# Loads ahead of their stage in a feed-forward and recurrent attention kernel

## The chip, the cores and the metric

The kernel runs on one core of a Trainium2 chip. Five engines work side by side, each through its own instruction queue in order: TensorE (PE, with its weight loads as PEld), VectorE (DVE), ScalarE (ACT), GpSimd (POOL), and SyncE (SP), which here only issues DMAs. They are ordered among each other by semaphores alone. The metric is the device time of one execution in microseconds (us), the median of several runs.

## What is computed

The input x is 4 x 1024 rows of 512 numbers. Two things are computed from its layer norm xn, and the output is x + s * silu(f):

```
xn = layernorm(x)
s  = gated delta rule attention: qkvz = xn @ w_qkvz.T, causal conv of 4 taps and silu on q, k, v,
     per head and step  S = S*exp(g); S += k (x) ((v - k@S)*beta); o = q@S
     s = rmsnorm(o * silu(z)) * norm_weight @ w_out.T
f  = feed-forward: routed = sigmoid(xn @ w_router + b_router) > 0.5
     h  = xn + (rmsnorm(xn)*n1 @ wv + bv) @ wo
     h2 = rmsnorm(h)*n2
     f  = where(routed, h + (silu(h2 @ w_gate) * (h2 @ w_up)) @ w_down, xn)
out = x + s * silu(f)
```

Everything is float32 but for some 16 bit intermediates in attention. The feed-forward width is 1408 (11 tiles of 128).

## The kernel before, in words

The program runs in two parts, one after the other. The functions are `feed_forward` and `attention`, both called from `program`.

**Feed-forward** works on 8 units of 512 rows (`UNITS_F`), each cut into 4 pieces of 128 rows (`NJ`). First the value and output weights are multiplied into one matrix (`pe_merge_weights`, L151 and L155 for the bias), which waits for both weights whole. Each unit then goes through an opening (`stats`, `normalise`, `router`: layer norm, mean square and router score, on VectorE), a front of three kinds of step per piece, and a back part. The front's steps are `columns` (PE transposes the normalised rows into `bank[0]`, ScalarE copies them out to `xt`, which also goes to DRAM for attention, L427), `attn` (PE multiplies by the merged matrix, L278; VectorE adds it into `h`, L288; ScalarE squares it, L297; GpSimd raises the mean to the power -1/2, L203) and `back` (VectorE scales the rows by that power, L304, in `dve_norm2`; PE transposes them, L313; VectorE evicts them into `h2t`, L322, and prepares `h`). The back part is 11 `gate` steps (gate product L347, silu on ScalarE L362, up product L352, product of both on VectorE L370) and 4 `down` steps (L383, selection on VectorE L392, silu L397, store to DRAM L457).

These steps are put into one list `order`, in which all engines work: the front of unit u is merged evenly with the gate steps of unit u - 1, and the down steps of unit u - 1 with the opening of unit u + 1. So in units 1 to 7 of the front, front steps and gate steps alternate; unit 0 has no gate steps to alternate with. Each engine runs its share of a step when it comes to it in the list. SP issues the loads and stores from a list of its own; it waits for a transfer or an engine where the code says so. At its end SP waits for its stores, the semaphores are cleared and all engines meet (L529).

**Attention** starts with a block of its own that loads three constants and fills `wlev` (L674 to L684). In the next block SP loads the first tile of columns, the small parameters, the weights of the first half of the heads in four kinds k, q, v, z (6 MB), the second tile and the output weights, and only then serves the loops. PE's first product there (L806) waits for tile 0 and the k weights. The order of all further work in this part comes from `planned`, a planner with a cost for every step (`TAKES`) and a due time for each; it runs 32 tiles of 256 rows (two groups of heads, four batches, four tiles). Row loads (`load_rows`) and stores serve the second group.

Of the kernel before, what the change touches and what calls it, by code (L numbers as in the profile page):

```python
# [99 lines left out]
def feed_forward(nc, bank, x, cst, w_router, b_router, norm1_w, wvt, bv, wo, norm2_w, w_gate, w_up, w_down, xt_d, g_d):  # L100


    with ExitStack() as ctx:
# [3 lines left out]
        def sem(name):  # L107
# [22 lines left out]
        sel = sb("sel", [P, 2, D])  # L130

        names = ["c_in", "r_in", "w_in", "g_in", "d_in", "z_set", "z_out", "h_set", "bvb", "wvo_ps", "wvo_sb", "cb_ps", "cb_sb",
                 "x_in0", "x_in1", "x_in2", "x_in3", "stat", "mvs", "var", "rst", "xnd", "sqd", "scr", "r1a", "r1d", "rtd", "kpt", "xc",
                 "trx", "xtd", "xt_out", "a_ps", "h_sb", "sq_sb", "r2a", "r2d", "h2s", "trh", "h2td", "xk", "hk",
                 "g_ps", "u_ps", "g_act", "hid_sb", "d_ps", "selw", "g_done", "g_out0", "g_out1"]
        s = {n: sem("f_" + n) for n in names}
        first, last = s[names[0]].num, s[names[-1]].num
# [20 lines left out]
        def act_merge_weights(act):  # L158
            act.wait_ge(s["c_in"], 16 * (1 + len(small)))
# [4 lines left out]
        def dve_spread_bias(dve):  # L164
            dve.wait_ge(s["c_in"], 16 * (1 + len(small)))
# [81 lines left out]
        def pe_columns(pe, u, j):  # L247

            n = NJ * u + j
            if n == 0:  # L250
                pe.wait_ge(s["c_in"], 16 * (1 + len(small)))
# [143 lines left out]
        def act_select(act, u, j):  # L395
# [4 lines left out]
        front = [("columns", 0), ("columns", 1), ("attn", 0), ("columns", 2), ("attn", 1), ("columns", 3), ("back", 0), ("attn", 2), ("back", 1), ("attn", 3),  # L400
                 ("back", 2), ("back", 3)]
        order = [(step, 0) for step in (("stats",), ("normalise",), ("router",))]
# [1521 lines left out]
```

## Time and profile before

| | |
|---|---|
| median of 3 runs | 4777.71 us (4777.23 to 4779.94) |
| profiled execution | 4782.79 us, span 4781.0 us |
| PE busy | 4586.8 us (96%) |
| PE weight loads | 3134.5 us (66%) |
| VectorE busy | 2680.7 us (56%) |
| ScalarE busy | 2348.9 us (49%) |
| GpSimd busy | 1387.1 us (29%) |
| mean granted clock of PE | 0.991 |
| HBM traffic | 79.09 MB read, 34.11 MB written, 24 GB/s over the span |

How the rows are read. A row of a timeline has the start in us, the duration in us, the engine (SPq is SP's DMA issues), the line of the kernel, the operation, output and inputs, shapes, and xN where N instructions of a kind are merged; in brackets stands the idle time of the engine before it and what ended that. A row of waits names the engine and line that waited, what for, the total in us, the number of waits and the longest. A window row has the stretch, its length, then busy us and number of instructions of PE, PEld, DVE, ACT and POOL, the granted PE clock (1.00 is full speed, 2.4 GHz, and 0.50 the lower of the two levels, 1.2 GHz), the mean busy share of the 16 DMA engines, and GB/s. The granted clock at the very start of the trace is shown as 1.00 until the first change is recorded. Ends of matmuls are modelled: each is shown a little longer than its slot. SP's duration is that of the issue; the landing is listed apart.

### The profile page before, as it was taken

The page shows a single profiled execution, that of the slowest core. Times are in us where ns is not written, and L with a number is a line of the kernel's source. Part 1 is how long each engine was busy: PE and PEld are TensorE (multiplying, and loading weights), DVE is VectorE, ACT ScalarE, POOL GpSimd, SP SyncE. Part 2 cuts the span into 40 slices and gives each one's busy share as a digit, 9 for nine tenths or more (in the row PEclk, how much of TensorE's full clock was granted, in tenths as well). Part 3 has the DMA queues.
Part 4 walks back from the last instruction along what each step waited for, and adds up shares of the span by engine and source line. Part 5 has one row for each costly group of instructions (what it writes and reads, how often), then busy time and mean ns, then how long its engine had stood idle before and what let it go on. Part 6 is the DMA issues. An engine that isn't in the chain of part 4 may idle for free.

```text
span 4781.0 us, 81715 instructions
## 1 busy us (share of the span) xinstructions
PE 4586.8 (96%) x30056; PEld 3134.5 (66%) x30056; DVE 2680.7 (56%) x6818; ACT 2348.9 (49%) x5714; POOL 1387.1 (29%) x1542
## 2 busy tenths in 40 slices
PE   7999999997899999999999999999999999999998
PEld 3444444443777777777777777777777777777775
DVE  3222222212666666666666666666676666667664
ACT  1000111101566656666666666666666666666664
POOL 1000000000233333333333333333343333434333
PEclk9999999998999999999999999999999999999998
DMA  3000000002000000000000001100000000010000
GB/s 132 19 27 25 22 24 27 18 9 94 6 10 10 10 12 10 10 10 10 10 10 17 10 28 45 34 23 23 29 26 23 23 23 23 23 37 23 23 19 30
DMA packets 72605, 118.46 MB, mean 25 GB/s; under 512 B 12432, under 2 KB 29456, under 8 KB 72208
## 3 DMA queue, kind: packets, MB, share of 16 engines
q1 hardware_dynamic: 72208, 113.22, 7.1%
q8 instruction: 242, 3.96, 0.4%
q14 instruction: 155, 1.27, 0.1%
HBM read 79.09 MB, written 34.11 MB: 24 GB/s over the span
## 4 chain that ended last, share of the span: by engine, by line
PE 63%; DVE 10%; issue 1%; ACT 1%; POOL 0%; SPq 0%; DMA 0%; DVEq 0%; POOLq 0%; ACTq 0%
PE bank L806 18%; PE bank L810 10%; PE bank L1169 9%; PE bank L1448 7%; DVE vraw L836 3%; PE bank L1086 2%; PE bank L1342 2%; PE bank L1356 2%; PE bank L1382 2%; PE bank L1294 2%; PE bank L1317 2%; PE bank L1070 1%; PE bank L945 1%; PE bank L1071 1%; PE bank L812 1%
## 5 line engine op out<-in xcount | busy, mean ns | idle before, releaser
L806 PE MATMUL bank<-xtile,wt 128*128 128x259 f32 x4096 | 1083.0, 396 | 79.2 <-DVE vraw L836 50.9
L806 PEld LDWEIGHTS bank<-xtile,wt 128*128 128x128 f32 x4096 | 725.5, 191 | 214.3 <-DVE vraw L836 81.1
L1228 ACT ACTIVATE xyinv<-bank 128x512 f16<-128x512 f32 x768 | 457.4, 596 | 365.0 <-PE bank L1169 362.5
L1206 DVE TENSOR_TENSOR wlev<-bank,mask 128x256 f16<-128x256 f32 x768 | 320.9, 420 | 469.6 <-PE bank L1169 467.0
L1448 PE MATMUL bank<-wot,xnt 128*128 128x512 f32 x1024 | 532.8, 611 | 0.9 <-ACT xnt L1441 0.8
L810 PE MATMUL bank<-wt,xtile 128*128 128x512 f32 x1024 | 523.4, 617 | 0.0
L836 DVE SCALAR_TENSOR_TENSOR vraw<-bank,taps,vraw 128x256 f32<-128x256 f32 x768 | 370.2, 482 | 126.7 <-ACT vraw L829 105.5
L370 DVE TENSOR_TENSOR hid<-bank,gate 128x512 f32<-128x512 f32 x88 | 60.9, 692 | 521.1 <-PE bank L352 521.1
L1146 POOL TENSOR_TENSOR kend<-ktok,bend 128x256 f32<-128x256 f32 x256 | 158.6, 640 | 636.3 <-issue 635.8
L1169 PEld LDWEIGHTS bank<-xyinv,lth 128*128 128x128 f16 x3584 | 220.7, 98 | 167.3 <-issue 108.5
L347 PE MATMUL bank<-h2t,wg_sb 128*128 128x512 f32 x704 | 318.4, 595 | 0.0
L352 PE MATMUL bank<-h2t,wu_sb 128*128 128x512 f32 x704 | 316.5, 592 | 0.0
L383 PE MATMUL bank<-wd_sb,hid 128*128 128x512 f32 x704 | 303.5, 592 | 0.9 <-DVE hid L370 0.9
L1121 POOL TENSOR_TENSOR ltm<-ltm,mask 128x512 f32<-128x512 f32 x128 | 148.2, 1158 | 501.5 <-DVE ltm L1104 501.5
L1169 PEld LDWEIGHTS bank<-wlev,xyinv 128*128 128x128 f16 x3072 | 187.1, 99 | 144.7 <-issue 95.0
L1169 PE MATMUL bank<-xyinv,lth 128*128 128x64 f16 (+1 forms) x3584 | 265.1, 197 | 0.9 <-ACT xyinv L1228 0.9
L829 ACT ACTIVATE vraw<-bank,taps 128x256 f32<-128x256 f32 x256 | 121.6, 475 | 282.7 <-PE bank L806 279.8
L1055 POOL TENSOR_TENSOR gm<-con,gdec 128x512 f32<-128x512 f32 x128 | 133.6, 1044 | 401.5 <-PE bank L1086 315.5
L352 PEld LDWEIGHTS bank<-h2t,wu_sb 128*128 128x128 f32 x704 | 133.8, 190 | 168.4 <-issue 168.4
L383 PEld LDWEIGHTS bank<-wd_sb,hid 128*128 128x128 f32 x704 | 133.1, 190 | 166.2 <-issue 166.2
L362 ACT ACTIVATE gate<-bank 128x512 f32<-128x512 f32 x88 | 52.6, 598 | 360.1 <-PE bank L347 360.1
L347 PEld LDWEIGHTS bank<-h2t,wg_sb 128*128 128x128 f32 x704 | 130.7, 191 | 146.0 <-issue 146.0
(179 smaller groups left out, 9327.0 us busy)
## 6 DMA issues: line engine op xcount, KB each, us to landing
xtile<-xt_scratch SPq DMA_DIRECT2D x32, 518.0 KB, 4.1
xn<-x SPq DMA_DIRECT2D x32, 256.0 KB, 5.3
xt_scratch<-xt SPq DMA_DIRECT2D x8, 1024.0 KB, 5.8
g_scratch<-sel SPq DMA_DIRECT2D x32, 256.0 KB, 2.0
wt<-w_qkvz SPq DMA_DIRECT2D x4, 2048.0 KB, 13.2
part_scratch<-prow SPq DMA_DIRECT2D x32, 256.0 KB, 2.1
prow<-part_scratch SPq DMA_DIRECT2D x32, 256.0 KB, 2.7
grow<-g_scratch SPq DMA_DIRECT2D x32, 256.0 KB, 3.5
```

What stands on the lines that cost most here:

```text
L347: i = pe.matmul(bank[2 + f % 2][:], wg_sb[:, k, f * P:(f + 1) * P], h2t[:, u % 2, k, :], start=(k == 0), stop=(k == KT - 1))
L352: i = pe.matmul(bank[4 + f % 2][:], wu_sb[:, k, f * P:(f + 1) * P], h2t[:, u % 2, k, :], start=(k == 0), stop=(k == KT - 1))
L383: i = pe.matmul(bank[6 + j % 2][:], hid[:, f, j * P:(j + 1) * P], wd_sb[:, f, :], start=(f == 0), stop=(f == FT - 1))
L806: j = pe.matmul(b_p[:, 0:WIN], wt[:, k, c:c + P], xtile[:, par, k, :], **st)
L810: j = pe.matmul(b_p[:], xtile[:, par, k, HALO + cc * P:HALO + (cc + 1) * P], w, **st)
L836: dve.scalar_tensor_tensor(out=acc, in0=tile_bank("product", prod_of[i])[:, tap:tap + TILE], scalar=taps[:, group(q), i, tap:tap + 1], in1 ...
L1121: pool.tensor_tensor(ltm[:], ltm[:], mask[:, M_NEG, :].unsqueeze(1).broadcast_to([P, HEADS, P]), ALU.subtract).then_inc(s["lti_sb"], 1)
L1146: i = pool.tensor_tensor(kend[:, r * REP:(r + 1) * REP], ktok[:, tile % 2, cc, m * KPB + r].unsqueeze(1).broadcast_to([P, REP, P]), bend[: ...
L1169: i = pe.matmul(dst[:, h * cols:(h + 1) * cols], lhsT(h), rhs(h), start=start and h == 0, stop=stop, skip_group_check=True)
L1206: dve.tensor_tensor(wlev[:, lv - 1].rearrange("p h (b t s) -> p h b t s", t=2, s=z)[:, :, :, 0, :], b_inv[p][:, 0:HEADS * P // 2].rearrang ...
L1228: act.activation(dst, b_inv[p][:].rearrange("p (a h b s) -> p a h b s", a=2, h=HEADS, s=z), ACT.Copy).then_inc(s[f"xy_sb{p}"], 1)
L1448: i = pe.matmul(b_o[:], xnt[:, h], wot[:, h], start=(h == 0), stop=(h == GV - 1))
```

## The change

- A set of tiles and semaphores that attention needs (`resident`) is now allocated around both parts: constants, masks, `nw`, the qkvz weights `wt`, two tiles of columns, `sel`, and the small parameters. The gate and up weights lie in the memory of `wt`, the value and output weights in that of `hid`, and attention's `xrow` and `grow` in that of `sel`.
- Value and output weights come in four slices of rows each, as the first DMAs; each slice pair has a semaphore `w_in{e}`. The three small vectors are issued after the first pair, and the load of x after the last. The merge runs over slices on the outside, so that all four banks finish during the last slice.
- Attention's constants are loaded right after x, its small parameters during unit 0, tiles 0 and 1 of the columns at the beginning of the last round of SP's loop (when all columns are in DRAM), and the weights of the first half after the last up product (`u_ps`), beside the last down products.
- The scaling of the rows (`dve_norm2`) is a step `scale` of its own, put right behind `attn`, and the front's order relative to the gate steps is written out by hand.
- The semaphore clear and the barrier between the parts are gone; so are SP's waits for its stores (row loads of the second group wait for `g_out`), and the block for the constants. VectorE makes its constants at the head of its attention program; GpSimd waits for them (`c_set`), and PE before the first level step with `lv == 1`.

```diff
+def resident(nc, ctx):
+    shapes = {"con": ([P, N_CONST, P], F32), "mask": ([P, N_MASK, P], F16), "nw": ([P, 1], F32), "wt": ([P, KT, GROWS], F32), "xtile": ([P, 2, KT, WIN], F32), "sel": ([P, 2, D], F32),
+              "wba": ([P, KT, GROUPS, 4 * GK], F32), "taps": ([P, GROUPS, 4 * GK, TAPS], F32), "dtb": ([P, GROUPS, GV], F32), "neg_a": ([P, GROUPS, GV], F32)}
+    r = {name: ctx.enter_context(nc.sbuf_tensor(name, shape, dtype)) for name, (shape, dtype) in shapes.items()}
+    for name in ("c_in", "wk_in", "wq_in", "wv_in", "wz_in", "wba_in", "small_in", "x_in0", "x_in1", "g_out0", "g_out1"):
+        r[name] = ctx.enter_context(nc.semaphore("a_" + name))
+    return r
...
+def load_weights(sp, r, w_qkvz, g, kind):
+    lo, hi = W_SPANS[kind]
+    sp.dma_start(r["wt"][:, :, lo:hi], w_qkvz[:, g * GROWS + lo:g * GROWS + hi].rearrange("(k p) n -> p k n", p=P)).then_inc(r[f"w{kind}_in"], 16)
+def load_columns(sp, r, xt_d, q):
+    b, i = divmod(q % HALF_TILES, TPB)
+    sp.dma_start(r["xtile"][:, q % 2], xt_d[:, :, b * PADT + i * TILE:b * PADT + i * TILE + WIN]).then_inc(r[f"x_in{q % 2}"], 16)
...
-        ident, zero = sb("f_ident", [P, P]), sb("f_zero", [P, D])
-        wvt_sb, wo_sb, bvb = sb("wvt_sb", [P, KT, D]), sb("wo_sb", [P, KT, D]), sb("bvb", [P, KT, P])
+        ident, zero = r["con"][:, C_ID, :], sb("f_zero", [P, D])
-        wg_sb, wu_sb = sb("wg_sb", [P, KT, FF]), sb("wu_sb", [P, KT, FF])
+        both = r["wt"][:].rearrange("p k n -> p (k n)")
+        wg_sb, wu_sb = (both[:, i * KT * FF:(i + 1) * KT * FF].rearrange("p (k f) -> p k f", k=KT) for i in range(2))
...
+        wvt_sb, wo_sb = hid[:, 0:KT, :], hid[:, KT:2 * KT, :]
+        sel = r["sel"]
...
         def pe_merge_weights(pe):
-            pe.wait_ge(s["w_in"], 32)
-            for k in range(KT):
-                for e in range(KT):
+            for e in range(KT):
+                pe.wait_ge(s[f"w_in{e}"], 32)
+                for k in range(KT):
                     i = pe.matmul(bank[2 + k][:], wvt_sb[:, e, k * P:(k + 1) * P], wo_sb[:, e, :], start=(e == 0), stop=(e == KT - 1))
-                i.then_inc(s["wvo_ps"], 1)
+                    if e == KT - 1:
+                        i.then_inc(s["wvo_ps"], 1)
...
-        front = [("columns", 0), ("columns", 1), ("attn", 0), ("columns", 2), ("attn", 1), ("columns", 3), ("back", 0), ("attn", 2), ("back", 1), ("attn", 3),
-                 ("back", 2), ("back", 3)]
+        front = ["gate", "gate", ("columns", 0), ("columns", 1), "gate", ("attn", 0), ("scale", 0), ("columns", 2), "gate", "gate", ("back", 0), ("attn", 1), ("scale", 1),
+                 ("columns", 3), "gate", "gate", ("back", 1), ("attn", 2), ("scale", 2), "gate", "gate", ("back", 2), ("attn", 3), ("scale", 3), "gate", "gate", ("back", 3)]
         for u in range(UNITS_F + 1):
-            lists = []
-            if u < UNITS_F:
-                lists.append([(step, u) for step in front])
-            if u:
-                lists.append([(("gate", f), u - 1) for f in range(FT)])
-            order += merged(*lists)
-            lists = []
-            if u:
-                lists.append([(("down", j), u - 1) for j in range(NJ)])
-            if u + 1 < UNITS_F:
-                lists.append([(step, u + 1) for step in (("stats",), ("normalise",), ("router",))])
-            order += merged(*lists)
+            f = 0
+            for step in front:
+                if step != "gate" and u < UNITS_F:
+                    order.append((step, u))
+                elif step == "gate" and u:
+                    order.append((("gate", f), u - 1))
+                    f += 1
+            order += merged([(("down", j), u - 1) for j in range(NJ)] if u else [], [(step, u + 1) for step in opening] if u + 1 < UNITS_F else [])
...
+                for e in range(KT):
+                    sp.dma_start(wvt_sb[:, e, :], wvt[e * P:(e + 1) * P, :]).then_inc(s[f"w_in{e}"], 16)
+                    sp.dma_start(wo_sb[:, e, :], wo[e * P:(e + 1) * P, :]).then_inc(s[f"w_in{e}"], 16)
+                    if e == 0:
+                        for dst, src in small:
+                            sp.dma_start(dst, src).then_inc(s["c_in"], 16)
                 load(0)
-                sp.dma_start(ident[:], cst[:, C_ID, :]).then_inc(s["c_in"], 16)
-                for dst, src in small:
-                    sp.dma_start(dst, src).then_inc(s["c_in"], 16)
+                load_constants(sp, r, cst, masks, norm_weight)
...
-                sp.dma_start(wvt_sb[:], kp(wvt)).then_inc(s["w_in"], 16)
-                sp.dma_start(wo_sb[:], kp(wo)).then_inc(s["w_in"], 16)
-                sp.wait_ge(s["w_in"], 32)
+                for e in range(KT):
+                    sp.wait_ge(s[f"w_in{e}"], 32)
+                sp.wait_ge(s["x_in3"], 16)
                 sp.dma_start(wg_sb[:], kp(w_gate)).then_inc(s["g_in"], 16)
                 sp.dma_start(wu_sb[:], kp(w_up)).then_inc(s["g_in"], 16)
                 load(1)
                 sp.wait_ge(s["g_in"], 32)
...
                 columns_out(0)
-                sp.wait_ge(s["d_in"], 16)
+                load_small(sp, r, conv_w, dt_bias, a_log, w_ba)
                 sp.wait_ge(s["z_set"], 1)
                 for dst, src in zeros:
                     sp.dma_start(dst, src).then_inc(s["z_out"], 16)
...
+                    if u == UNITS_F:
+                        sp.wait_ge(s["z_out"], 16 * len(zeros))
+                        sp.wait_ge(s["xt_out"], 16 * UNITS_F)
+                        for q in range(2):
+                            load_columns(sp, r, xt_d, q)
+                        sp.wait_ge(s["u_ps"], FT * UNITS_F)
+                        for kind in "kqvz":
+                            load_weights(sp, r, w_qkvz, 0, kind)
                     for j in range(NJ):
                         sp.wait_ge(s["g_done"], NJ * (u - 1) + j + 1)
                         row = (u - 1) * FTILE + j * P
                         sp.dma_start(g_d[row:row + P, :], sel[:, j % 2, :]).then_inc(s[f"g_out{j % 2}"], 16)
-                sp.wait_ge(s["z_out"], 16 * len(zeros))
-                sp.wait_ge(s["xt_out"], 16 * UNITS_F)
-                for p in range(2):
-                    sp.wait_ge(s[f"g_out{p}"], 8 * NJ * UNITS_F)
...
+                    elif kind == "scale":
+                        dve_norm2(dve, u, *i)
                     elif kind == "back":
-                        dve_norm2(dve, u, *i)
                         dve_back(dve, u, *i)
                         dve_keep(dve, u, *i)
...
-        nc.gpsimd.sem_clear(range(first, last + 1))
-        nc.all_engine_barrier()
...
+        def dve_constants(dve):
+            dve.memset(mhalf[:], -0.5).then_inc(c_set, 1)
+            for lv in range(LEVELS - 1):
+                dve.tensor_copy(wlev[:, lv], mask[:, M_ID, :].unsqueeze(1).broadcast_to([P, HEADS, P])).then_inc(c_set, 1)
+            dve.wait_ge(c_set, LEVELS)
...
             if lv == 1:
                 pe.wait_ge(s[f"y1_sb{p}"], u + 1)
+            if n == 0 and lv == 1:
+                pe.wait_ge(c_set, LEVELS)
...
+            if c == HALF_CHUNKS:
+                for p in range(2):
+                    sp.wait_ge(s[f"g_out{p}"], 8 * CHUNKS // GROUPS)
...
-                load_tile(sp, 0)
-                load_small(sp)
-                load_products(sp, 0, "kqvz")
-                load_tile(sp, 1)
                 load_out(sp, 0)
...
+                pool.wait_ge(c_set, LEVELS)
                 for kind, *i in order["pool"]:
```

The functions `load_constants` and `load_small` of the new version issue the same DMAs as the lines L674 to L676 and L691 to L694 of before. The attention functions take their tiles from `resident`; nothing else in them differs.

## Rows read from the trace of the kernel before

**Rows 1.** Windows by stage, all engines.
```profile
0.00:16.76 16.76, 0.00 (x1) 0.01 (x1) 7.60 (x22) 0.00 (x0) 2.03 (x8) 1.00 0.63 208
16.76:70.08 53.32, 39.94 (x108) 19.03 (x109) 19.75 (x43) 9.08 (x17) 10.81 (x16) 0.91 0.62 212
70.08:1138.80 1068.72, 1034.87 (x2557) 463.47 (x2556) 233.79 (x458) 109.67 (x204) 74.04 (x110) 1.00 0.06 21
1138.80:1161.83 23.03, 0.15 (x2) 0.04 (x1) 2.30 (x9) 2.13 (x3) 0.00 (x0) 0.57 0.49 125
1161.83:4781.00 3619.17, 3511.80 (x27392) 2651.98 (x27392) 2417.23 (x6288) 2227.98 (x5490) 1300.20 (x1408) 0.99 0.07 22
```

**Rows 2.** Waits of PE from 64 to 1150 us: total, times, longest.
```profile
PE bank L313 <- DVE h L304: 33.0, 28, 1.2
```

**Rows 3.** Timeline from 0 to 39 us, DVE, PE and SP.
```profile
0.73 1.81 SPq L422 DMA_DIRECT2D xn<-x  x4
...
7.57 2.46 DVE L210 BATCH_NORM_STATS2 stats<-xn 128x6 f32<-128x512 f32 x4
...
11.90 1.91 DVE L222 TENSOR_SCALAR xn<-xn,mv,rstd 128x512 f32<-128x512 f32 x4 [1.58 <-POOL rstd L179]
...
16.76 16.84 PE L151 MATMUL bank<-wo_sb,wvt_sb 128*128 128x512 f32 x32 [16.76 <-DMA wo_sb<-wo]
...
36.87 0.60 PE L256 MATMUL bank<-f_ident,xn 128*128 128x128 f32 x4
...
37.07 0.69 DVE L170 COPY cbias<-bank 128x512 f32<-128x512 f32 x1 [17.11 <-PE bank L155]
...
38.71 3.60 PE L278 MATMUL bank<-wvo,xt 128*128 128x512 f32 x8
```

**Rows 4.** DMA issues from 0 to 9 us: count, KB each, us to landing.
```profile
xn<-x SPq DMA_DIRECT2D x4, 256.0 KB, 3.4
```

**Rows 5.** Windows in two other cuts, all engines.
```profile
69.00:73.60 4.60, 4.42 (x9) 2.36 (x10) 4.25 (x13) 1.88 (x2) 0.00 (x0) 0.50 0.01 4
...
1160.00:1180.00 20.00, 16.69 (x62) 12.86 (x63) 9.12 (x20) 5.55 (x9) 0.00 (x0) 0.85 1.04 399
```

**Rows 6.** Timeline of the end of unit 0.
```profile
53.44 3.60 PE L278 MATMUL bank<-wvo,xt 128*128 128x512 f32 x8
...
57.18 0.75 DVE L288 SCALAR_TENSOR_TENSOR h<-bank,r,h 128x512 f32<-128x512 f32 x1 [1.66 <-PE bank L278]
...
59.04 0.55 POOL L203 TENSOR_TENSOR r<-r,mhalf 128x1 f32<-128x1 f32 x1
...
69.17 1.11 PE L256 MATMUL bank<-f_ident,xn 128*128 128x128 f32 x4 [6.67 <-DVE xn L222]
```

**Rows 7.** Timeline of one stall in unit 1's front.
```profile
253.97 3.60 PE L352 MATMUL bank<-h2t,wu_sb 128*128 128x512 f32 x8
...
258.22 0.48 DVE L304 TENSOR_SCALAR h<-h,r 128x512 f32<-128x512 f32 x1
...
258.75 0.66 PE L313 MATMUL bank<-f_ident,h 128*128 128x128 f32 x4 [1.18 <-DVE h L304]
...
259.44 0.69 DVE L322 TENSOR_TENSOR h2t<-bank,n_sb 128x512 f32<-128x512 f32 x1 [0.75 <-PE bank L313]
```

**Rows 8.** Timeline of SP, two stores of columns.
```profile
251.36 0.52 SPq L427 DMA_DIRECT2D xt_scratch<-xt  x1
...
387.49 0.52 SPq L427 DMA_DIRECT2D xt_scratch<-xt  x1
```

**Rows 9.** Timeline from the last down products to the first attention product.
```profile
1100.94 38.01 PE L383 MATMUL bank<-wd_sb,hid 128*128 128x512 f32 x88 [0.87 <-DVE hid L370]
...
1140.53 0.32 SPq L457 DMA_DIRECT2D g_scratch<-sel  x1
...
1143.63 0.33 SPq L674 DMA_DIRECT2D con<-cst  x1
...
1161.83 5.79 PE L806 MATMUL bank<-xtile,wt 128*128 128x259 f32 x16 [22.88 <-DMA wt<-w_qkvz]
```

More of the change, by code:

```diff
@@ L129, in feed_forward @@
         hid = sb("hid", [P, FT, FTILE])
-        sel = sb("sel", [P, 2, D])
-        names = ["c_in", "r_in", "w_in", "g_in", "d_in", "z_set", "z_out", "h_set", "bvb", "wvo_ps", "wvo_sb", "cb_ps", "cb_sb",
+        wvt_sb, wo_sb = hid[:, 0:KT, :], hid[:, KT:2 * KT, :]
+        sel = r["sel"]
+        names = ["c_in", "r_in", *(f"w_in{e}" for e in range(KT)), "g_in", "d_in", "z_set", "z_out", "h_set", "bvb", "wvo_ps", "wvo_sb", "cb_ps", "cb_sb",
                  "x_in0", "x_in1", "x_in2", "x_in3", "stat", "mvs", "var", "rst", "xnd", "sqd", "scr", "r1a", "r1d", "rtd", "kpt", "xc",
                  "trx", "xtd", "xt_out", "a_ps", "h_sb", "sq_sb", "r2a", "r2d", "h2s", "trh", "h2td", "xk", "hk",
-                 "g_ps", "u_ps", "g_act", "hid_sb", "d_ps", "selw", "g_done", "g_out0", "g_out1"]
+                 "g_ps", "u_ps", "g_act", "hid_sb", "d_ps", "selw", "g_done"]
         s = {n: sem("f_" + n) for n in names}
-        first, last = s[names[0]].num, s[names[-1]].num
+        s.update({n: r[n] for n in ("g_out0", "g_out1")})
         kp = lambda a: a.rearrange("(k p) n -> p k n", p=P)
@@ L158, in act_merge_weights @@
         def act_merge_weights(act):
-            act.wait_ge(s["c_in"], 16 * (1 + len(small)))
+            act.wait_ge(s["c_in"], 16 * len(small))
             for k in range(KT):
@@ L250, in pe_columns @@
             if n == 0:
-                pe.wait_ge(s["c_in"], 16 * (1 + len(small)))
+                pe.wait_ge(r["c_in"], 48)
             pe.wait_ge(s["xnd"], n + 1)
@@ L591, in merged, with attention @@
     return [step for _, _, step in sorted(at, key=lambda x: x[:2])]
-def attention(nc, bank, x, cst, masks, w_qkvz, w_ba, conv_w, dt_bias, a_log, norm_weight, w_out, xt_d, g_d, part_d, out):
+def attention(nc, bank, r, x, w_qkvz, w_out, xt_d, g_d, part_d, out):
     with ExitStack() as ctx:
@@ L628, in attention @@
         xnt = sb("xnt", [P, GV, P])
-        xrow, grow, prow = sb("xrow", [P, D]), sb("grow", [P, D]), sb("prow", [P, D])
+        xrow, grow, prow = r["sel"][:, 0, :], r["sel"][:, 1, :], sb("prow", [P, D])
         pout, yout = prow, grow
@@ L1466, in pool_out @@
             pool.wait_ge(s["po_sb"], c + 1)
-            pool.tensor_tensor(yout[:], pout[:], grow[:], ALU.mult).then_inc(s["yg_sb"], 1)
+            pool.tensor_tensor(yout, pout[:], grow, ALU.mult).then_inc(s["yg_sb"], 1)
             pool.wait_ge(s["yg_sb"], c - HALF_CHUNKS + 1)
-            pool.tensor_tensor(yout[:], yout[:], xrow[:], ALU.add).then_inc(s["yo_sb"], 1)
+            pool.tensor_tensor(yout, yout, xrow, ALU.add).then_inc(s["yo_sb"], 1)
         def rows(c):
@@ L1476, in load_rows @@
             sp.wait_ge(s["stored"], 16 * c)
-            for dst, src in ((prow, part_d), (grow, g_d), (xrow, x)):
-                sp.dma_start(dst[:], src[rows(c), :]).then_inc(s["rows_in"], 16)
+            if c == HALF_CHUNKS:
+                for p in range(2):
+                    sp.wait_ge(s[f"g_out{p}"], 8 * CHUNKS // GROUPS)
+            for dst, src in ((prow[:], part_d), (grow, g_d), (xrow, x)):
+                sp.dma_start(dst, src[rows(c), :]).then_inc(s["rows_in"], 16)
         def store(sp, c):
@@ L1485, in store @@
                 sp.wait_ge(s["yo_sb"], c - HALF_CHUNKS + 1)
-                sp.dma_start(out[rows(c), :], yout[:]).then_inc(s["stored"], 16)
+                sp.dma_start(out[rows(c), :], yout).then_inc(s["stored"], 16)
         unit_lanes, tile_lanes = {}, {}
@@ L1811, in _ @@
             def _(dve):
+                dve_constants(dve)
                 dve_rates(dve)
@@ L1878, in program @@
         bank = [ctx.enter_context(nc.psum_tensor(f"bank{i}", [P, 512], F32)) for i in range(8)]
-        feed_forward(nc, bank, x, cst, w_router, b_router, norm1_w, wvt, bv, wo, norm2_w, w_gate, w_up, w_down, xt_d, g_d)
-        attention(nc, bank, x, cst, masks, w_qkvz, w_ba, conv_w, dt_bias, a_log, norm_weight, w_out, xt_d, g_d, part_d, out)
+        r = resident(nc, ctx)
+        feed_forward(nc, bank, r, x, cst, masks, w_qkvz, w_ba, conv_w, dt_bias, a_log, norm_weight,
+                     w_router, b_router, norm1_w, wvt, bv, wo, norm2_w, w_gate, w_up, w_down, xt_d, g_d)
+        attention(nc, bank, r, x, w_qkvz, w_out, xt_d, g_d, part_d, out)
 _INS = ["w_qkvz", "w_ba", "conv_w", "dt_bias", "A_log", "norm_weight", "w_out"]
```

73 lines of the change are left out of this document (29 added, 44 removed).

## The prediction

> **What bounds the kernel now.** I read the busy time by stage first. [rows 1] cut the span at five points: the wait for the first weights, unit 0 of the feed-forward part, its units 1 to 7, the change from one part to the other, and attention. TensorE (PE) is busy for 1034.87 of 1068.72 us in units 1 to 7 and for 3511.80 of 3619.17 us in attention, so it is the bound in both, and time is won only where it stands still: 16.76 us at the start, 13.4 us in unit 0, about 34 us in the units and 22.9 us at the change. The waits say what these are. In the units nearly all of it is one wait, the transposes of the scaled rows (L313) for the scaling of them (L304), 33.0 us in 28 pieces [rows 2]. The timelines of the start, of unit 0, of one such stall and of the change carry the four terms below.
>
> **Term 1, the start.** PE merges the value and output weights from 16.76, when both megabytes have landed, and reaches the first column transposes (call them c0) at 36.87: 20.1 us, of which some 3 are the half clock of its first matmuls (32 in 16.84 us [rows 3], against the 0.43 us each of term 3). The change issues the first slice pair as the first two DMAs, and the merge goes slice by slice. The four loads of x, 256 KB each as every slice is, went out at 0.73 [rows 3] and took 3.4 us from issue to landing [rows 4]; so the first pair, issued by about 1.2, lands near 4.3 with the count of its semaphore. If no later slice is late, c0 comes at 4.3 + 20.1 = 24.4, 12.5 us earlier. A slice pair feeds PE for 3.4 us at full clock and 6.9 at half; the last is needed near 17. At the poorest rate of a row, 208 GB/s over the whole start [rows 1], 2.1 MB are there by 11. So the slices are not the limit. x now comes behind them: 3.1 MB are there by 16 at 208 GB/s, and by 9 at the 399 GB/s of the weight stream at the change [rows 5]; I take 12. VectorE then needs 0.6 us for the last statistics, 1.9 from there to the first normalised row (7.57 + 2.46 to 11.90), and 8.1 from that to the end of the router work (11.90 to 19.96, which is 37.07 less its 17.11 of idle time), after which it copies the bias that the first value/output product (a0) needs [rows 3]. That is 23 at my value, hidden by the merge, and 27 at the poor rate, which would put a0 at 28 in place of 26.2. Term: -12.5, with -10.7 and -13 as ends. The gate and up weights are asked for when slices and x have landed, near 13 where it was 16.7, and are needed at 56: covered.
>
> A page speaks against this part. The Trainium skill ("DMA: Bandwidth & Descriptors", Rules for kernel authors) advises transfers of a megabyte or more and calls those below 64 KB mostly overhead; the eight slices are 256 KB, where there were two of 1 MB. Taken at the 138 GB/s that its table has for 64 KB, as an estimate, the 2 MB would need 15 us and the last slice would still come about when PE asks for it. The x loads of the same size, down in 3.4 us [rows 4], show nothing of such a rate.
>
> **Term 2, unit 0.** Without gate steps to lie between, moving the scaling ahead has a price here: VectorE and PE now do product, row scaling and back-transpose strictly one after the other. From the rows of the last product: start of the product to VectorE's update 3.74 us (53.44 to 57.18), to the end of the power on GpSimd 2.41, hand-over 0.05, scaling to the transposes 0.53 (258.22 to 258.75), transposes 0.50 (0.66 less a tail of 0.16): 7.2 us for each of four [rows 6, 7]. The last transposes start at 28.4 after a0; 0.69 to the eviction, 0.69 in it (259.44) and 0.1 more, and unit 0's first gate product can start: 29.9 after a0. Before, a0 at 38.71 to unit 1's first columns at 69.17 is 30.5, and PE was then at half clock until 73.6, which cost another 2.2 us: 32.7 [rows 3, 6]. The wait for unit 1's normalised rows (6.67) is gone, since two gate steps of 6.9 us now lie ahead of those columns, where VectorE needs 4.3 us to its first normalised row (7.57 to 11.90) and a little more for what it still has of unit 0. The clock decides what remains. In the chain PE idles about 3 us after each 3.9 of work; in the trace it was down after the 6.67 us wait (0.50 at 69 to 73.6 [rows 5]) and stood at 0.91 on average over 16.76 to 70.08, in which PE was busy for three quarters [rows 1]. Between no loss and every matmul of the stage at half clock (16 us of work, +16, and 2 in the first gate) I take 4, nearer to none, since no idle stretch here is half as long as that wait. Term: 29.9 + 4 - 32.7 = +1.2, from -3 to +15.
>
> The Trainium skill ("TensorE: Matmul & The Clock Gate", HAM oscillation) describes such a loop, bursts of matmuls with waits between, as one that falls back to half clock at every wait and pays for it in each burst. By that rule the stage would lie at the upper end, and it is a rival below.
>
> **Term 3, units 1 to 7.** A unit takes 136.13 us (251.36 to 387.49 from one store of columns to the next) [rows 8]. The up product of 253.97 has 8 matmuls of 0.43 us (38.01 less 3.60 over 80 more of them [rows 7, 9]) and a modelled tail of 0.16; its slot ends at 257.41; the transposes start at 258.75. VectorE does the product with the gate (it waits for that same up product), and only then the scaling: 1.34 us, four times a unit. In the new order the scaling stands right behind the value/output product, with two gate steps before its transposes, so it is ready (3.3 us after the product's end against 13.8): -5.36 a unit. New is, first, that the columns 0 and 1 stand side by side and share a bank: from the first of them to the product behind both 1.84 us (36.87 to 38.71 [rows 3]), where two sets of four transposes without a wait would take 0.92 (0.60 and 0.66 in the rows, less the tail: taken as 0.46 each), +0.92. Second, the down products wait for the last gate product's eviction; in the last unit that showed as 0.87 of idle time and the tail of 0.16 [rows 9]; with 0.46 of transposes between, +0.57. The wait that VectorE gains at each scaling is 1.7 us (57.18 + 0.75 to 59.6); behind it stands the product with the gate for a step that PE ends 7 us after the value/output product, so some 4 us of slack remain, and ScalarE's squares and GpSimd's power have nothing long ahead of them. Unit: 132.26. Term: 7 x -3.87 = -27.1. Ends: -29 (the transposes lose their slow start too, 0.03 to 0.06 each) and 0 (rival).
>
> **Term 4, the change.** PE's last down product ends at 1138.8 and the first attention product starts at 1161.83. What lies between: the last selection and its store (issued until 1140.85), its landing, a semaphore clear with two barriers, constants from 1143.63, then tile, small loads and weights one after another [rows 9]. All of these loads now are issued before: constants at the start, small ones in unit 0, two tiles after unit 6's stores, and 6 MB of weights once the last gate step is through, a microsecond before the down products' start at 1100.94. At 399 GB/s [rows 5] they take 16 us, beside down products of 38.01 us. Stores of the selection are queued behind them on SP; the buffer of the first is needed again by the third selection, three of four down products or 28.5 us later: free. What stays is selection, ScalarE, the last store's issue and the block's exit; by the rows that is 1140.85 plus part of the 2.8 us to 1143.63, a landing and a clear now left out. I take 1141.7 (1141.1 to 1144): PE starts 20.1 earlier. VectorE's constants (they are within the 2.30 us of its work in this stretch [rows 1]) run beside the first product. That product ran at half clock, 16 matmuls in 5.79 us, where full clock would need some 3.4 (an estimate: 259 columns against the 512 of 0.43 us); after 3 us instead of 23 of idle time the clock may hold, worth 0 to 2.5, taken as 1. Term: -21.1.
>
> **At nothing:** eleven more small issues of SP in the first 60 us (SP has no one waiting until 115); `sel` as home of `xrow` and `grow`; the waits on g_out, long fulfilled at chunk 32; the planner's order, whose costs are untouched. Uncovered, the SP issues would cost 6 us.
>
> **Sum.** -12.5 + 1.2 - 27.1 - 21.1 = -59.5 us. The profiled execution took 4782.79 (span 4781.0), so it would take 4723.3; it lay 5.1 above the median of 4777.71, and the median comes to **4718**.
>
> **Rivals.**
> 1. The clock falls in each wait of unit 0 and stays down into attention (for: by the rows of term 2 PE is idle nearly half of the stage; against: work of 3.9 us between). +12 from term 2, +1 from term 4: 4731. Chance 0.15.
> 2. The start stays bound by loads: x behind the weights, or slices trickling in (for: 208 GB/s; against: 3.4 us landings). Half to all of term 1 goes: 4724 to 4731. Chance 0.08.
> 3. The moved scaling does not free PE: VectorE's new 1.7 us waits push the gate evictions late, so that term 3 is lost and 28 x 0.4 us come on top (for: VectorE is strictly in order; against: 4 us of slack). 4718 + 27 + 11 = 4756. Chance 0.06.
> 4. The change of parts is only half closed, because stores sit behind 6 MB or the exit costs more: 4725. Chance 0.05.
> 5. Slower than before: attention itself paces differently with its tiles at other places in memory. It has 3619 us [rows 1]; it decides from 59.5 us, 1.6% of that, 1.9 us in each of 32 tiles. Nothing in the profile speaks for it: same instructions, same order. At 2.5% it would give 4808. Chance 0.03.
> Forecast: 0.63, for itself 4709 to 4727.
>
> **Numbers.** The range takes in rivals 1, 2 and 4: 4704 to 4736, which leaves out 3 and 5 and about a tenth on the edges. 0.2%, the least that can be told from no change here, is 9.6 us. Faster 0.96, same 0.01, slower 0.03.
>
> **What would show it.** PE's first matmul near 4.3 and c0 near 24.4 (term 1); unit 0's first gate product near 56 to 62, with the granted clock of 26 to 60 above 0.8 (term 2); no wait of L313's successor on the scaling in units 1 to 7, one of 0.8 us for ScalarE's columns instead, and 132.3 us between stores of columns (term 3); some 3 us between the last down product and the first attention product (term 4); attention within 5 us of 3619. Wrong would be it with a first matmul after 8, a unit above 134, or an attention stage longer by more than 10 us.

## The result, and the profile after

The changed kernel takes 4718.83 us (median of 4 runs, 4716.38 to 4724.52); in the same comparison the kernel before takes 4777.48 us. The ratio is 0.9878, with an interval of 0.9861 to 0.9895. The forecast was 4718. The two profiled executions took 4782.79 and 4719.77 us, a difference of 63.0: the one of before lay 5.3 us above its median, the one of after 0.9. So the terms below add up to 63 us, not to 59.

Lines of the kernel after that the rows name: L190 is the merge and L195 its bias, L296 the transposes of the columns and L304 ScalarE's eviction of them, L318 the value/output product, L344 the scaling, L353 the transposes of the scaled rows and L362 their eviction, L387 the gate and L392 the up product, L410 the product of both, L423 the down products, L455 the feed-forward block itself, L824 attention's first products. In kernels that the experiments edit, some of these stand one or two lines lower.

The windows of the kernel after, cut as in [rows 1] (wait for the first weights, unit 0, units 1 to 7 with the last down products, the change, attention):

```profile
0.00:4.22 4.22, 0.00 (x0) 0.00 (x0) 0.00 (x0) 0.00 (x0) 0.75 (x6) 1.00 0.50 130
4.22:57.79 53.57, 40.32 (x105) 18.44 (x105) 22.81 (x51) 10.04 (x18) 10.81 (x16) 0.97 0.84 278
57.79:1100.00 1042.21, 1032.30 (x2560) 466.56 (x2560) 238.94 (x471) 107.43 (x203) 75.32 (x112) 1.00 0.08 28
1100.00:1102.46 2.46, 0.00 (x0) 0.03 (x1) 0.87 (x3) 0.82 (x2) 0.00 (x0) 0.97 0.04 14
1102.46:4718.00 3615.54, 3505.92 (x27392) 2647.63 (x27392) 2418.52 (x6295) 2229.01 (x5492) 1300.35 (x1408) 0.99 0.06 20
```

PE's idle time went from 16.8 to 4.2 us at the start, from 34 to 10 us in the units and from 22.9 to 2.5 us at the change. In unit 0 it stayed at 13. The three largest waits of PE from 60 to 1115 us, engine and line, what for, total, number and longest:

```profile
PE bank L296 <- ACT xt L304: 5.9, 7, 0.9
PE bank L423 <- DVE hid L410: 3.9, 8, 0.9
PE bank L824 <- PEq L455: 2.5, 1, 2.5
```

The 33.0 us of [rows 2] are gone altogether. In their place stand the two small waits that the prediction named, on ScalarE's columns (L296, seven times) and on the last gate product's eviction (L423), and the exit of the feed-forward block (L455). The timeline of the kernel after, start and unit 0:

```profile
4.22 16.88 PE L190 MATMUL bank<-hid 128*128 128x512 f32 x32 [4.22 <-DMA hid<-wo]
...
5.91 2.30 SPq L460 DMA_DIRECT2D xn<-x  x4
...
11.86 2.73 DVE L250 BATCH_NORM_STATS2 stats<-xn 128x6 f32<-128x512 f32 x4 [6.68 <-DMA xn<-x]
...
13.96 0.38 SPq L480 DMA_DIRECT2D wt<-w_gate  x1
...
24.37 0.60 PE L296 MATMUL bank<-con,xn 128*128 128x128 f32 x4
24.57 0.69 DVE L210 COPY cbias<-bank 128x512 f32<-128x512 f32 x1
...
26.22 3.60 PE L318 MATMUL bank<-wvo,xt 128*128 128x512 f32 x8
...
32.96 0.66 PE L353 MATMUL bank<-con,h 128*128 128x128 f32 x4 [2.71 <-DVE h L344]
33.45 5.29 PE L318 MATMUL bank<-wvo,xt 128*128 128x512 f32 x8
...
42.39 3.60 PE L318 MATMUL bank<-wvo,xt 128*128 128x512 f32 x8
...
49.12 0.66 PE L353 MATMUL bank<-con,h 128*128 128x128 f32 x4 [3.13 <-DVE h L344]
49.61 3.60 PE L318 MATMUL bank<-wvo,xt 128*128 128x512 f32 x8
...
57.79 5.39 PE L387 MATMUL bank<-h2t,wt 128*128 128x512 f32 x8 [0.78 <-DVE h2t L362]
```

And from the timeline of the same execution, two stores of columns one unit apart, then the change:

```profile
238.09 0.52 SPq L465 DMA_DIRECT2D xt_scratch<-xt  x1
...
370.37 0.52 SPq L465 DMA_DIRECT2D xt_scratch<-xt  x1
...
1061.12 2.38 SPq L128 DMA_DIRECT2D wt<-w_qkvz  x4
...
1061.96 38.01 PE L423 MATMUL bank<-wd_sb,hid 128*128 128x512 f32 x88 [0.87 <-DVE hid L410]
...
1102.46 5.35 PE L824 MATMUL bank<-xtile,wt 128*128 128x259 f32 x16 [2.49 <-PEq L455]
```

| term | forecast | measured | from |
|---|---|---|---|
| 1, start | -12.5 | -12.5 | first columns at 24.37, before 36.87 |
| 2, unit 0 | +1.2 | +0.7 | 31.57 + 1.8 of half clock in the first gate product, against 32.7 |
| 3, units | -27.1 | -27.0 | 132.28 us a unit, before 136.13 |
| 4, change | -21.1 | -20.4 and -3.6 | down products to first attention product 40.50, before 60.89; attention 3615.54, before 3619.17 |

### The profile page after: what moved, and what is told of

It is laid out like the page before. It is cut to its first block and busy times, and to the rows that moved or that the text cites. A ratio compares the mean times of both kernels' runs of the same rounds, so it can differ in the third digit from the quotient of the medians.

```text
span 4718.0 us, 81696 instructions
## 1 busy us (share of the span) xinstructions
PE 4578.5 (97%) x30056; PEld 3132.7 (66%) x30056; DVE 2681.1 (57%) x6818; ACT 2347.3 (50%) x5714; POOL 1387.2 (29%) x1542
## 5 line engine op out<-in xcount | busy, mean ns | idle before, releaser
L824 PE MATMUL bank<-xtile,wt 128*128 128x259 f32 x4096 | 1080.0, 396 | 58.8 <-DVE vraw L854 50.5
L824 PEld LDWEIGHTS bank<-xtile,wt 128*128 128x128 f32 x4096 | 723.7, 191 | 192.6 <-DVE vraw L854 80.8
L828 PE MATMUL bank<-wt,xtile 128*128 128x512 f32 x1024 | 523.4, 617 | 0.0
L410 DVE TENSOR_TENSOR hid<-bank,gate 128x512 f32<-128x512 f32 x88 | 60.9, 692 | 485.5 <-PE bank L392 485.5
L387 PE MATMUL bank<-h2t,wt 128*128 128x512 f32 x704 | 318.3, 595 | 0.8 <-DVE h2t L362 0.8
L392 PE MATMUL bank<-h2t,wt 128*128 128x512 f32 x704 | 316.5, 592 | 0.0
L423 PE MATMUL bank<-wd_sb,hid 128*128 128x512 f32 x704 | 304.0, 593 | 3.9 <-DVE hid L410 3.9
L423 PEld LDWEIGHTS bank<-wd_sb,hid 128*128 128x128 f32 x704 | 133.1, 190 | 170.7 <-issue 170.7
L392 PEld LDWEIGHTS bank<-h2t,wt 128*128 128x128 f32 x704 | 133.8, 190 | 168.4 <-issue 168.4
L387 PEld LDWEIGHTS bank<-h2t,wt 128*128 128x128 f32 x704 | 132.7, 191 | 159.9 <-issue 158.9
```

The lines of the kernel that those rows point to most:

```text
L387: i = pe.matmul(bank[2 + f % 2][:], wg_sb[:, k, f * P:(f + 1) * P], h2t[:, u % 2, k, :], start=(k == 0), stop=(k == KT - 1))
L392: i = pe.matmul(bank[4 + f % 2][:], wu_sb[:, k, f * P:(f + 1) * P], h2t[:, u % 2, k, :], start=(k == 0), stop=(k == KT - 1))
L423: i = pe.matmul(bank[6 + j % 2][:], hid[:, f, j * P:(j + 1) * P], wd_sb[:, f, :], start=(f == 0), stop=(f == FT - 1))
L824: j = pe.matmul(b_p[:, 0:WIN], wt[:, k, c:c + P], xtile[:, par, k, :], **st)
L828: j = pe.matmul(b_p[:], xtile[:, par, k, HALO + cc * P:HALO + (cc + 1) * P], w, **st)
```

## The experiments

All of them are edits of the changed kernel. Their medians are set beside its 4718.83, but they were taken in three comparisons, each with its own runs of the kernel before: 4783.19 us beside `late_weights`, `x_first`, `whole_first` and `scale_in_back`, 4778.76 beside `old_front`, `unit0_order`, `columns_apart` and `warm`, 4778.0 beside the rest. The first of these is 5.7 us above the 4777.48 of the result, so differences of medians of a few microseconds carry little. Of the edited kernels all but `scale_in_back`, `old_front` and `both_orders` have ratios whose intervals meet the 0.9861 to 0.9895 of the changed kernel; for those the reading rests on the rows of one profiled execution each.

**The scaling and the order (terms 2 and 3).** `scale_in_back` keeps the hand-written front and moves only the scaling back into the `back` step:

```
-                    elif kind == "scale":
-                        dve_norm2(dve, u, *i)
                     elif kind == "back":
+                        dve_norm2(dve, u, *i)
```

> The changed kernel with the scaling of the rows done at the head of the back step again; the hand-written order of the front is kept. My theory: what paid in units 1 to 7 is that the scaling no longer stands behind the product with the gate; so the stall of 1.34 us comes back four times a unit, a unit takes 137.6 instead of 132.27 us, unit 0 stays as it is (nothing stands between there), and the time is 4718.8 + 37.5 = 4756. Rival (the gain comes from the new order, two gate steps ahead of each back step): no change within 3 us.

It took 4754.52 us (ratio to before 0.9945, 0.993 to 0.9959). The waits of PE and two stores of columns of this kernel:

```profile
PE bank L353 <- DVE h L344: 36.1, 29, 3.1
```

```profile
111.67 0.52 SPq L465 DMA_DIRECT2D xt_scratch<-xt  x1
...
248.86 0.52 SPq L465 DMA_DIRECT2D xt_scratch<-xt  x1
```

The stall is back (33 us in 28 pieces and one of 3.1 that belongs to unit 0), and a unit takes 137.19 us. The order alone gives nothing; in it a unit is even 1.06 us longer than before, with the new wait on ScalarE's columns (7 times 0.84 us in its waits) as the largest part. The 0.4 us a unit that I expected too much is the wait before the down products (L423): its waits show it once, in the last unit, where the kernel after has it eight times.

`old_front` restores order and scaling of before, and leaves the early loads in:

```
-            f = 0
-            for step in front:
-                ...
+            lists = []
+            if u < UNITS_F:
+                lists.append([(step, u) for step in front])
+            ...
```

> The changed kernel with the order of the feed-forward steps and the scaling inside the back step as they were before; all early loads and the sliced merge stay. My theory (terms 2 and 3 are the order's alone, and the early loads have no part in them): a unit takes 136.1 us instead of 132.27, 27 us in all, and unit 0 is a little shorter, by 0.7 us between its first value/output product and its first gate product at full clock: 4718.8 + 27.0 - 0.7 = 4745. Rival (the terms are not additive, part of the gain of the order came from earlier loads): 4735 or less.

4745.69 us (0.9931, 0.9916 to 0.9945), a unit 136.14. So terms 2 and 3 together are 26.9 us in medians, and they do not lean on the early loads.

`unit0_order` gives unit 0 a list of its own:

```
+        first = [("columns", 0), ("columns", 1), ("attn", 0), ("scale", 0), ("columns", 2), ("attn", 1), ("columns", 3),
+                 ("back", 0), ("scale", 1), ("attn", 2), ("back", 1), ("scale", 2), ("attn", 3), ("back", 2), ("scale", 3), ("back", 3)]
...
-            for step in front:
+            for step in (front if u else first):
```

> The changed kernel with a list of its own for unit 0: product 1 ahead of back 0, product 2 ahead of back 1, product 3 ahead of back 2, each scaling ahead of the transposes by one product. My theory: the price of unit 0 is a chain of four times product, scaling, transposes, 7.2 us each; with products between, only the last stall of 2.8 us is left, the first gate product comes 20.4 us after the first value/output product instead of 31.6, and the clock does not fall: 4718.8 - 11.2 - 1.5 = 4706. Rival (unit 0 is bound by loads or by what VectorE has to do for unit 1, so that the wait moves behind it): 4715 to 4719.

4707.31 us (0.9851, 0.9836 to 0.9866). PE in the timeline of this kernel, from the first value/output product to the first gate product:

```profile
25.52 3.60 PE L318 MATMUL bank<-wvo,xt 128*128 128x512 f32 x8
...
44.82 0.66 PE L353 MATMUL bank<-con,h 128*128 128x128 f32 x4 [3.21 <-DVE h L344]
46.27 5.35 PE L387 MATMUL bank<-h2t,wt 128*128 128x512 f32 x8 [0.78 <-DVE h2t L362]
```

20.75 us instead of 31.57, one stall on the scaling instead of four. The clock half of the expectation failed in one place: all four products run at full clock, but the first gate product still does not (5.35 us for 8 against 3.60).

`columns_apart` puts a gate step between columns 0 and columns 1:

```
-        front = ["gate", "gate", ("columns", 0), ("columns", 1), "gate", ...
+        front = ["gate", ("columns", 0), "gate", ("columns", 1), "gate", ...
```

> The changed kernel with a gate step between columns 0 and columns 1 (gate, columns 0, gate, columns 1, gate, ...). My theory: the wait of PE for ScalarE's eviction of the shared bank, 0.9 us in each of seven units, goes: 4718.8 - 6.3 = 4712.5. Rival (unit 1's first rows are not normalised after one gate step, and the wait comes back there): up to 3 us of it return, 4715.5.

4713.75 us (0.9863, 0.9848 to 0.9878). A unit takes 131.22 us (239.55 to 370.77 between stores of columns), 1.06 less, 7.4 in all; no wait came back in unit 1. The median alone, 5.1 us lower, could not show it. Its timeline holds one row that the kernel after does not have:

```profile
26.03 3.67 PE L318 MATMUL bank<-wvo,xt 128*128 128x512 f32 x8 [1.20 <-DVE cbias L210]
```

Here the bias was late. VectorE copied it at 25.20, 0.6 us later than in the kernel after, because x landed later (its first use is at 12.67, in the kernel after at 11.86); and the merge took 15.39 us instead of 16.88, so PE was ready 1.5 us earlier (first columns at 22.82). x, behind the slices, held PE up by 1.2 us in this execution.

**The start (term 1).** `x_first` issues x and the small vectors ahead of the slices, `whole_first` keeps the weights first but as two loads of 1 MB:

```
 x_first:                                       whole_first (the merge waits for w_in0 alone):
+                load(0)                        +  sp.dma_start(wvt_sb, kp(wvt)).then_inc(s["w_in0"], 16)
+                for dst, src in small: ...     +  sp.dma_start(wo_sb, kp(wo)).then_inc(s["w_in0"], 16)
                 for e in range(KT): ...        -  for e in range(KT): ...
-                load(0)                           load(0)
```

> The changed kernel with x and the small vectors issued ahead of the eight weight slices. My theory: slicing and order each carry a part of term 1. The first slice pair is issued at about 5.4 and lands near 8.7, so the merge starts 4.5 us later than at 4.22, the first column transposes come near 28.9 and the time is 4723.3. Rival a: order is everything (x ahead costs the whole 12.5 us): merge at 16.7, 4731. Rival b: slices behind x trickle in and stop the merge in between: merge starts near 9 but takes more than the 16.9 us of before.

> The changed kernel with value and output weights as two loads of 1 MB, still the first to be issued; the merge keeps its loop over slices but waits once for both. My theory: at about 400 GB/s both are there near 8.5, so the merge starts 4.3 us later than with slices and the time is 4723.1. Rival (large transfers run so much faster that slicing wins nothing): both land by 5.5, 4720 or less. If they land as slowly as in the kernel before (8.7 and 10.8 us from issue) the merge starts at 12 and the time is 4726.5.

4727.05 us (0.9886, 0.987 to 0.9903) and 4724.17 us (0.9884, 0.9869 to 0.9899). The merge in the timeline, of `x_first` and of `whole_first`:

```profile
8.53 16.34 PE L190 MATMUL bank<-hid 128*128 128x512 f32 x32 [8.53 <-DMA hid<-wo]
```

```profile
8.99 16.77 PE L190 MATMUL bank<-hid 128*128 128x512 f32 x32 [8.99 <-DMA hid<-wo]
```

The merge starts 4.3 us later behind x and 4.8 us later with whole weights; both were expected at 4.3 to 4.5. The columns follow at 28.14 and 29.04. The rest of term 1 (16.76 to about 8.8) comes with either of the two alone. `x_first` is 8 us slower in its median and not 4. The clock of unit 0 (below) may be a part: from its first value/output product to the first gate product it took 33.74 us, `whole_first` 31.57. The kernel before in the same comparison, 5.7 us above its other median, may be another: by the ratio to it, `x_first` would be at 4723.0 on the scale of the result, where 4723.3 was expected.

The 2 MB are there at 8.99 in two pieces. In eight pieces the last, issued at 5.43, took 5.7 us and was there at 11.1; the merge, which needs it last, ran 16.88 us and was not stopped. The Trainium skill ("DMA: Bandwidth & Descriptors", Rules for kernel authors) asks for a megabyte or more per transfer where the greatest bandwidth is the aim. The 11.1 against 8.99 does not speak against that, though three small loads stood among the slices and no run separates the causes. Here a smaller first piece decided, and the rate of the whole did not.

**The change (term 4).** `late_weights` loads tiles and weights at the head of attention again; `late_both` also the small parameters:

```
-                load_small(sp, r, conv_w, dt_bias, a_log, w_ba)        # late_both only
-                        ...
-                        for q in range(2):
-                            load_columns(sp, r, xt_d, q)
-                        ...
-                            load_weights(sp, r, w_qkvz, 0, kind)
 (attention)
+            load_columns(sp, r, xt_d, 0)
+            load_small(sp, r, conv_w, dt_bias, a_log, w_ba)        # late_both only
+            for kind in "kqvz":
+                load_weights(sp, r, w_qkvz, 0, kind)
+            load_columns(sp, r, xt_d, 1)
```

> The changed kernel with the two column tiles and the 6 MB of attention weights loaded at the head of attention again; constants and small parameters stay early, the clear and the barrier stay out. My theory: the change of parts was bound by a chain in which the weights were only the last link (issue to first product 6.2 us in the kernel before, 1155.60 to 1161.83); so the first attention product comes about 6.7 us later than in the changed kernel, near 3 + 6.7 us after the last down product, and the time is 4725.5. Rival a: the weights were the whole of it, 20 us, then 4739. Rival b: taking out barrier, clear and constants was all, then 4719.

> The changed kernel with the column tiles, the weights and also the small parameters loaded at the head of attention, in the order of the kernel before. My theory: the loads stand in one chain on SP, so that the nine small issues (5.9 us from 1149.67 to 1155.56 in the kernel before) add to what the late weights alone showed (9.27 us of idle time ahead of the first attention product): 15.2 us of idle time there, and 4719 + 12.7 = 4732. The rest of the 22.9 us of before (7.7 us) then is the constants' block, the clear and the landing of the last store. Rival (the small issues overlap with the weights' transfer, only the transfer counts): idle time of 9 to 10 us, 4726.

4728.74 us (0.9889, 0.9874 to 0.9903) and 4734.52 us (0.9906, 0.989 to 0.9923). First attention product in the timeline, of `late_weights` and of `late_both`:

```profile
1111.08 5.52 PE L825 MATMUL bank<-xtile,wt 128*128 128x259 f32 x16 [9.27 <-DMA wt<-w_qkvz]
```

```profile
1118.79 10.07 PE L825 MATMUL bank<-xtile,wt 128*128 128x259 f32 x32 [15.28 <-DMA wt<-w_qkvz]
```

With the 2.49 of after and the 22.88 of before [rows 9] this cuts the 20.4 us: 6.8 are tile and weights, 6.0 the nine small issues ahead of them, 7.6 the block of constants, the clear, the barriers and the landing of the last store, which no run takes apart. The late weights were the last link of a chain in which each link cost its own time. The medians are 3 us above what was expected in each case; the idle times are not. Why is not settled. Both profiled executions had more slow products in unit 0 than the one of after, but that of `late_weights` took 4725.19 us, which is what was expected; and its median was taken beside a kernel before of 4783.19.

`warm` keeps PE busy over the exit of the block:

```
                     elif kind == "down":
                         pe_down(pe, u, *i)
+                for k in range(5):
+                    pe.matmul(bank[0][:, 0:256], wvo[:, k % KT, 0:P], wvo[:, k % KT, 0:256], start=True, stop=True)
```

> The changed kernel with five extra matmuls of 256 columns (some 2.1 us of PE work, into a bank that nobody reads) behind the last down product. My theory: PE's first attention product ran at half clock because PE stood still for 2.5 us at the change; filled, it starts at the same time and takes 16 matmuls in 3.8 instead of 5.35 us, 1.6 us less, 4717.2. Rival (the clock falls there for another reason, or it falls later in the first tile anyway): no change in that row, 4718.8.

4716.5 us (0.9868, 0.9851 to 0.9884), which is no difference from 4718.83 that these runs can tell. From the timeline of this kernel:

```profile
1104.50 3.74 PE L826 MATMUL bank<-xtile,wt 128*128 128x259 f32 x16 [0.45 <-PEq L455]
...
1125.95 3.17 PE L826 MATMUL bank<-xtile,wt 128*128 128x259 f32 x8
```

The row came out as expected: 3.74 us instead of 5.35. But the product at 1125.95 took 3.17 us where the kernel after has 1.92, and a later one 3.44 against 2.02. Counted from the first product, PE reaches the pair of products at 1156.82 after 52.3 us, in the kernel after (1154.66) after 52.2. What the first product won was gone by then in this execution. That the filling caused the later slow products is not shown: without it, the other executions of the new layout reach this pair after 52.2 to 53.7 us, and in five of them the product at this place is as slow (3.62 to 3.66). Nor is it shown that the stage gained nothing: from its first product to the end this execution took 3612.1 us, the shortest of twelve (up to 3616.6). A gain of 1.6 us is smaller than this scatter.

**Together.** `both_orders` has the two orders at once, `after_again` is the changed kernel in the same comparison.

> The changed kernel with the order of its own for unit 0 and with a gate step between columns 0 and columns 1. My theory: the two gains are at different places and add up: 11.5 from unit 0 and 6.3 from the columns, so 4718.8 - 17.8 = 4701. Rival (with a shorter unit 0, unit 1's rows are not normalised after a single gate step): a new wait of 1 to 3 us at unit 1's first columns, 4703.

> The changed kernel as it is, for a comparison with the same runs of the kernel before: 4719, 58 to 60 us below. Every theory expects the same.

4701.22 us (0.9838, 0.9824 to 0.9853) against 4719.98 us (0.9881, 0.9866 to 0.9895): the intervals of the ratios don't meet. It beats both kernels, by 76.8 and 18.8 us. A unit takes 131.22 us, and the first columns of unit 1 follow a single gate step without a wait:

```profile
46.72 5.40 PE L387 MATMUL bank<-h2t,wt 128*128 128x512 f32 x8 [0.78 <-DVE h2t L362]
51.95 3.60 PE L392 MATMUL bank<-h2t,wt 128*128 128x512 f32 x8
55.39 0.60 PE L296 MATMUL bank<-con,xn 128*128 128x128 f32 x4
```

## Why the prediction was right

**The sum** hit within a microsecond, and part of that is luck. Of one profiled execution it forecast 4723.3 and this was 4719.77; the 3.6 us that attention was shorter, which it had at nothing, were made up by the position of the two profiled executions over their medians, 5.3 and 0.9 us, where 5.1 was taken for both. The mechanisms held.

**Term 1** held to 0.1 us in the row. That too is a near thing: ten executions start with the slices, their first columns come at 22.82 to 24.37, and the kernel after is the latest of them, since the merge, in part at half clock, took 15.39 to 16.88 us. The condition held only just. The first of the four x loads was used at 11.86, but the last, 6.3 us after its issue, landed near 13.9 and not at the 12 that I took (SP, which waits for it, goes on at 13.96); so VectorE ended the router work at 24.52 and not at 23. Its copy of the bias was done at 25.26, 1 us ahead of the product. In `columns_apart` it was 1.2 us late: part of rival 2 happened there, at a tenth of the term.

**Term 2.** The chain of 7.2 us is there (42.39 to 49.61 is 7.22). The clock fell once in the chain (5.29 us) and once at the first gate product (5.39), 3.5 us together, where I took 4. A fall in every wait is not what this trace shows: of the three products behind a wait on the scaling two ran at full clock, after waits of 2.71 and 3.13 us. The loop of the Trainium skill ("TensorE: Matmul & The Clock Gate", HAM oscillation), which slows in every round, has waits that are longer than its work; here they were shorter (about 3 us after 3.9 of work), so that it bears on this chain less than the prediction made of it. Of eight other profiled executions with this chain the last three products were slow once in one, twice in five, and three times in two. From the first value/output product to the first gate product all nine took 31.57 to 36.68 us, where 29.9 would be full clock: 1.7 us for one slow product, up to 6.8 for three. Their mean is 34.0, and the profiled execution of after, one of the two shortest, flatters the term: +0.7 there, but about +3 in the mean. Rival 1 was therefore not an alternative to the forecast but, in its first half, its scatter; its second half, a low clock from there into attention, did not come (the mean granted clock was 1.00 from 57.79 to 1100). `unit0_order` and `both_orders`, without the chain, bear this out in part: their four products ran at full clock, and `unit0_order` lay within 1.8 us over four runs, where the changed kernel spread over 8.1; `both_orders` still spread over 5.1.

**Term 3** held in each of its parts: `scale_in_back` gives back the stalls alone (rival 3, VectorE's new waits, never reached PE), and `columns_apart` the first of the two new waits, priced at 0.92 and measured at 1.06. The second, before the down products, showed as 0.43 us of idle time (3.9 in all, with 0.87 in the last unit); with the tail of 0.16 that is 0.59, priced at 0.57.

**Term 4** was right in place and size, and `late_weights` and `late_both` show that all links counted. One value in it was taken wrongly and did not matter: the clock did not hold over 2.5 us of idle time, the first product ran at half clock as before. Something like the -1 came from elsewhere, by luck. Later in the first tile a product took half the time that it took before (first row after, second before):

```profile
1125.11 1.92 PE L824 MATMUL bank<-xtile,wt 128*128 128x259 f32 x8
```

```profile
1186.09 3.66 PE L806 MATMUL bank<-xtile,wt 128*128 128x259 f32 x8
```

PE reaches its z products (L828, before L810) 1.3 us earlier, counted from the first product. But the change did not bring this: of the twelve executions with the new layout seven reach that point after 56.6 to 56.9 us, as after does, and five after 57.4 to 58.1, where before has 58.0. The other 2.3 us of attention's -3.6 lie spread over 3500 us. The twelve had 3612.1 to 3616.6 us from the first product to the end, so attention did not become slower (rival 5 is out); whether it became faster, one execution of before, and one that lay 5.3 us above its median, can't tell.

## What to carry to other kernels

An instruction that is ready early but stands behind a wait in its engine's queue costs its consumer the whole wait: move it ahead of that wait, and check that what is then queued behind it has slack. A list of steps that is good when two stages overlap can be a poor one where a stage runs alone (31.57 us in unit 0, 20.75 with a list of its own), so the first unit deserves its own. And a gap between two parts is a chain of loads, issues, barriers and landings; price each link, and move them all, since one that is left keeps its own share (6.8, 6.0 and 7.6 us here).

## What the runs showed of the hardware that was not expected

- PE filled over the block's exit ran its next product at full clock (3.74 us), but in that execution slow products turned up 20 us later, and PE reached the end of the first tile no sooner. One execution can't say whether the one brought the other.
- After a stall of 3.1 to 3.2 us and one of 0.8 the first gate product ran in part at half clock in every profiled execution with the hand-written front (5.35 to 5.77 us for 8 matmuls that take 3.60 at full clock), whether the work before it had run fast or not (5.35 in `unit0_order`, 5.39 in the kernel after).
- A first pair of 256 KB loads landed 3.1 us after the second of them was issued at 1.17 (4.22 to the first matmul), where a pair of 1 MB took 7.8 (1.22 to 8.99). The eighth slice took 5.7 us from its issue.
